# Adding the columns four apart on GpSimd instead of VectorE in a convolution with log-polar pooling, on one Trainium2 core

## What is computed

```python
# masks: 12 bins (2 radius levels x 6 angles) of a 9x9 window, each an average
y = conv(x per channel, masks)             # 12 pooled planes per channel
out = conv(planes arranged 4x3, w_conv1)   # = sum over channels and 12 bins
out = out + conv(x, w_center) + b_center
mean, var = out.mean((0, 2, 3)), out.var((0, 2, 3))
out = (out - mean) * rsqrt(var + 1e-5) * gamma + beta
return relu(out + x)
```

## Time and profile before

| | before |
|---|---|
| runs (3) | median 1686.37 us, 1686.28 to 1686.71 us |
| profiled execution, its own time | 1686.6 us |
| its span in the trace | 1684.8 us |
| mean granted TensorE clock | 0.949 |
| busy: PE / DVE / ACT / POOL | 1489.2 / 1531.3 / 645.3 / 2.7 us |
| phase 1 | to about 1533 us; phase 2 is the rest |

### The profile page before, as it was taken

The page is one execution under the profiler, slowest core; times in us unless marked ns, Lnnn a source line. Parts: engine busy times, 40 slices in busy tenths (PEclk is TensorE's granted clock), DMA queues, the critical chain, the costliest instruction groups (busy, mean ns, idle before and its releaser), DMA issues.

```text
span 1684.8 us, 21919 instructions
## 1 busy us (share of the span) xinstructions
PE 1489.2 (88%) x8468; PEld 1476.5 (88%) x8468; DVE 1531.3 (91%) x1455; ACT 645.3 (38%) x689; POOL 2.7 (0%) x21
## 2 busy tenths in 40 slices
PE   6899999999999999999999999999999999993000
PEld 6899999999999999999999999999999999993000
DVE  8999999999999999999999999999999999995423
ACT  3234343343333434334333343433433334434423
POOL 0000000000000000000000000000000000000000
PEclk8999999999999999999999999999999999997555
DMA  2010111001111011100111101111011110149999
GB/s 110 20 38 29 38 38 38 21 27 38 38 38 38 29 38 38 38 29 19 38 38 38 38 29 38 38 38 37 11 38 38 38 38 29 38 159 421 425 424 382
DMA packets 28615, 129.54 MB, mean 77 GB/s; under 512 B 3520, under 2 KB 3520, under 8 KB 28608
## 3 DMA queue, kind: packets, MB, share of 16 engines
q1 hardware_dynamic: 23744, 103.77, 17.0%
q10 hardware_dynamic: 4864, 25.69, 3.7%
HBM read 78.88 MB, written 50.58 MB: 77 GB/s over the span
## 4 chain that ended last, share of the span: by engine, by line
PE 50%; DVE 27%; issue 11%; SPq 5%; ACT 4%; DMA 3%; DVEq 0%; ACTq 0%
PE acc L625 17%; PE acc L627 16%; PE acc L626 16%; DVE pooled_split L403 6%; DVE pooled L402 6%; DVE inner_split L403 5%; SPq L266 3%; ACT inner_split L324 3%; DVE box L402 2%; DVE y_stage L402 2%; DVE row L402 2%; DMA phase<-x 2%; SPq L263 2%; DMA out<-phase 1%; ACT phase L394 0%
## 5 line engine op out<-in xcount | busy, mean ns | idle before, releaser
L334 ACT ACTIVATE pooled_split<-pooled 128x1456 fp32r<-128x1456 f32 x192 | 273.4, 1425 | 608.0 <-DVE pooled L402 608.0
L403 DVE TENSOR_TENSOR pooled_split<-pooled,pooled_split 128x1456 fp32r<-128x1456 f32 x192 | 317.4, 1667 | 0.3 <-ACT pooled_split L334 0.3
L625 PE MATMUL acc<-inner_split,w_first 128*128 128x406 f32 (+1 forms) x640 | 225.7, 353 | 36.3 <-DVE y_stage L402 25.0
L625 PE MATMUL acc<-pooled_split,w_first 128*128 128x364 f32 x768 | 253.6, 330 | 2.4 <-DVE pooled_split L403 2.4
L625 PE MATMUL acc<-pooled_split,w_outer 128*128 128x364 f32 x768 | 252.3, 329 | 1.1 <-DVE pooled_split L403 1.1
L626 PE MATMUL acc<-pooled_split,w_first 128*128 128x364 f32 x768 | 252.6, 329 | 0.0
L627 PE MATMUL acc<-pooled_split,w_first 128*128 128x364 f32 x768 | 252.5, 329 | 0.0
L626 PE MATMUL acc<-pooled_split,w_outer 128*128 128x364 f32 x768 | 252.2, 328 | 0.0
L627 PE MATMUL acc<-pooled_split,w_outer 128*128 128x364 f32 x768 | 251.8, 328 | 0.0
L627 PE MATMUL acc<-inner_split,w_first 128*128 128x406 f32 (+1 forms) x640 | 222.8, 348 | 0.0
L625 PE MATMUL acc<-inner_split,w_inner 128*128 128x406 f32 (+1 forms) x640 | 221.2, 346 | 1.1 <-DVE inner_split L403 1.1
(11 more groups left out here) (82 smaller groups left out, 2200.7 us busy)
## 6 DMA issues: line engine op xcount, KB each, us to landing
x_pad<-x SPq DMA_DIRECT2D x64, 392.0 KB, 3.3
y_dram<-y_stage SPq DMA_DIRECT2D x31, 784.0 KB, 5.0
phase<-y_dram SPq DMA_DIRECT2D x30, 784.0 KB, 28.3
phase<-x SPq DMA_DIRECT2D x30, 784.0 KB, 30.5
out<-phase ACTq DMA_DIRECT2D x30, 784.0 KB, 16.0
w_stage<-w_raw SPq DMA_DIRECT2D x2, 896.0 KB, 7.7
out<-x_pad ACTq DMA_DIRECT2D x2, 784.0 KB, 20.4
w_stage<-w_raw SPq DMA_DIRECT2D x2, 768.0 KB, 9.1
```

The costliest lines, as they stand in the source:

```text
L334: nc.scalar.activation(view(pooled_split, 2 * j * PAIR, (1, PAIR)), view(pooled, (PAIRS * c + j) % 2 * PAIR, (1, PAIR)), ACT.Copy)\
L403: sub = lambda out_, a, b: nc.vector.tensor_tensor(out_, a, b, ALU.subtract)
L625: nc.tensor.matmul(place, hi_w, hi_in, start=start, stop=False)
```

## The change

The add of the columns four apart leaves DVE's queue and stands in POOL's. There, add_ends waits for the image (x_loaded), for the short sums of the step before (pooled_ready, they read the tile ends), and for row3 of this step (row3_ready); then it adds and signals ends_ready. The semaphore x_used goes: SP's load of the next image waits for ends_ready in its place (row3 is the last of DVE's reads of x_pad in a step, so ends_ready, which comes behind row3_ready, covers them all). DVE's wait for ends_ready moves from before box4 to before the short sums.

```diff
--- before.py
+++ after.py
@@ -167,7 +167,6 @@
         zeroed = sem("zeroed")
         warmed_up = sem("warmed_up")
         x_loaded = [sem(f"x_loaded{c}") for c in range(CH)]
-        x_used = sem("x_used")
         d_ready = sem("d_ready")
         v_ready = sem("v_ready")
         inner_hi_ready = sem("inner_hi_ready")
@@ -232,6 +231,22 @@
                 nc.gpsimd.memset(edge, 0.0).then_inc(zeroed, 1)
                 n += 1
             assert n == ZEROED
+            pool.wait_ge(zeroed, ZEROED)
+
+            def add_ends(image):
+                for c in range(CH):
+                    s = CH * image + c
+                    first, second = (view(x_pad, c * X_PAD + (column + 2) * H, (H, W), (1, H)) for column in (-2, 2))
+                    pool.wait_ge(x_loaded[c], 16 * (image + 1))
+
+                    wait_from_one(pool, pooled_ready, PAIRS * s)
+                    pool.wait_ge(row3_ready, s + 1)
+                    nc.gpsimd.tensor_tensor(view(ends, 2, (ENDS_H, W), (1, H)), first, second, ALU.add)\
+                        .then_inc(ends_ready, 1)
+
+            add_ends(0)
+            with pool.Fori(1, IMAGES) as image:
+                add_ends(image)
 
         @block.sync
         def _(sp):
@@ -249,7 +264,7 @@
             def image_steps(image, first=False, last=False):
                 if not last:
                     for c in range(CH):
-                        sp.wait_ge(x_used, CH * image + c + 1)
+                        sp.wait_ge(ends_ready, CH * image + c + 1)
                         load_x(image + 1, c)
                 if not first:
                     sp.wait_ge(y_ready, CH * image + FREE)
@@ -533,8 +548,6 @@
                     dve.wait_ge(row2_ready, s + 1)
                     add(view(row3, 1, (ROW3_H, W + 2), (1, H)), view(row2, 4, (ROW2_H, W + 2), (1, H)),
                         columns(0, 1, W + 2)).then_inc(row3_ready, 1)
-                    add(view(ends, 2, (ENDS_H, W), (1, H)), columns(-2, 1, W), columns(2, 1, W))\
-                        .then_inc(ends_ready, 1)
 
                     dve.wait_ge(row3_ready, s + 1)
                     add(view(row3v, 2, (ROW3V_H, W + 2), (1, H + 1)), view(row3, 0, (ROW3_H, W + 2), (1, H + 1)),
@@ -550,8 +563,6 @@
                         if c == 0:
                             transform_weights(1)
 
-                    dve.wait_ge(ends_ready, s + 1)
-                    nc.vector.sem_inc(x_used, 1)
                     dve.wait_ge(row3v_ready, s + 1)
                     add(view(box4, 0, (BOX4_H, W + 2), (1, H + 3)), view(row3v, 0, (ROW3V_H, W + 2), (1, H + 3)),
                         view(row3v, 2, (ROW3V_H, W + 2), (1, H + 3))).then_inc(box4_ready, 1)
@@ -563,6 +574,7 @@
                     dve.wait_ge(box3_ready, s + 1)
                     pooled_sums(s, c, 1, box3, 4, 4 * BOX3_H - 4, BOX3_H, row2, 8, 5 * ROW2_H - 8, ROW2_H)
                     lo_of_pooled(s, c, 0)
+                    dve.wait_ge(ends_ready, s + 1)
                     short_sum(s, c, 0)
                     short_sum(s, c, 1).then_inc(pooled_ready, 1)
                     lo_of_pooled(s, c, 1)
```

## The result

The changed kernel takes 1748.15 us (median of 4 runs, 1748.0 to 1748.25) against 1686.36 us; the ratio is 1.037, with an interval of 1.035 to 1.038. It is slower by 61.8 us where 1745 was forecast. The profiled execution took 1748.0 us, its span is 1746.2 us.

The account below looks back on a forecast made before the run. A wait loop through PE and DVE bound the kernel at 46.72 us an image; DVE's own loop would take over at 48.57. 53.7 us over 29 periods plus 4.8 ahead, on 1686.6, gave 1745 us, range 1688 to 1773.

Parts of the forecast that it names:

- The mechanism: DVE's instructions with two SBUF inputs near row3v: each stands still for POOL's whole add, 1.5 to 2 us a step; chance 0.60.
- loop A: Image period through DVE, holding both steps' adds: 46.39 us before the change, forecast 48.57 after, then setting the pace.
- loop B: Image period through PE's wait for take_y, holding one step's add: 46.72 us and binding before, forecast 47.81 after.
- What is removed: The 64 adds of 0.969 us on DVE's queue: a step was to save 0.77 us, not 0.97.
- e: What DVE loses per POOL add, near row3v: forecast 1.86 us, between 0 and 2.31.
- hand-over: Passing between POOL and DVE at a stop: 0.12 us, counted once on top of POOL's 1.74 us add.
- The sum: Period 1.85 us longer, 53.7 us over 29 periods; 4.8 us ahead of them; 58.5 us together.
- head: The part ahead of 134.91 us, where DVE sets the pace in five steps: forecast 4.8 us longer.
- Rival 1: POOL's and DVE's SBUF reads go side by side, e = 0: period 45.95 us, 1660 us in all; chance 0.18.
- Rival 2: DVE's back-to-back reads keep POOL out until DVE waits for ends_ready: e = 1.98, 1753 us; chance 0.16.
- Rival 3: DVE is only slowed, e between 0.66 and 0.87, so the two moves cancel: 1686 us; chance 0.06.
- Waits and queues moved: add_ends's waits, SP's later load and store, DVE's moved wait for ends_ready: forecast to cost 0.

## Why the prediction was right, point by point

**The mechanism** was right in what it says of DVE: DVE is stopped by POOL's reading, in the place named (behind row3v), 1.5 to 2 us a step, and loop A takes over from loop B. What it left out is the clock. By the rule of the Trainium skill, "SBUF — State Buffer", section "Who interferes with whom", DVE with two SBUF inputs contends with a GpSimd instruction that reads, not with one that only writes, and a DVE instruction with at most one SBUF input, outside the modes that use both of its port pairs, doesn't contend. The runs agree on all three: 1.68 us with the add, 0 with the write, 0 beside the takes.

**What is removed** was right: row3 to row3v is 1.06 us (734.27 to 735.33), so a step saves 0.77.

**e** was forecast at 1.86 and is 1.68 + 0.07 = 1.75. POOL's own duration, forecast at 1.74, is 1.88 where nothing holds it; not all of it stops DVE. The skill's "GPSIMD Engine Reference", section 3.1, gave an estimated 1.72 by proportion, 8% under the 1.88 measured. The hand-over of 0.12 that I added is in no row. The 0.07 of the second wait ahead of the short sums is, and I had put that wait at nothing.

**Loop A** was overestimated. I took the idle of 0.34 us out of it, but an instruction that doesn't wait also overlaps the one before by 0.09, so without the wait the loop is 46.39 - 0.09 = 46.30. With that the measured stops give every period: 46.30 + 2 x (1.68 - 0.77 + 0.07) = 48.26 (measured 48.26); with DVE adding twice 46.30 + 2 x 0.885 = 48.07 (48.07).

**The sum.** 29 periods longer by 1.54 us are 44.7 us, where I had 53.7. The clock adds 8 x 1.55 = 12.4, where I had 0: I named it as what would bring the result above 1745 but gave it no price. The head gives 139.01 - 134.91 = 4.1, forecast 4.8; the stretch behind the last steady take_y 0.2, forecast 0. Together 61.4 us, the difference of the spans. So 1745 came out close by luck: two terms erred in opposite directions: e and loop A by 9.0 too much, the clock by 12.4 too little.

**Rival 1** (reads side by side, 1660 us) is refuted by the stops; its number, though, is the right floor within 2 us (1662.16 without an add), and an arrangement that keeps the reads apart nearly gets there. **Rival 2** didn't happen in the changed kernel; when the columns are halved, DVE's back-to-back reads do keep POOL out for seven instructions in every second step, though not until DVE waits for ends_ready. **Rival 3**, no change, didn't happen with the add; a copy of one operand, which is half of the reading, comes near it, with a stop of 0.65 us against the 0.77 saved, 1684.03 us.

**Waits and queues moved**: nothing but the 0.07 us a step above (the kernel without the add has a period of 46.03, loop B's 45.95 and this wait).

## What to carry to other kernels

Before an elementwise operation goes from VectorE to GpSimd, ask what VectorE runs at that moment: beside an instruction that reads two SBUF tiles the add here cost VectorE 1.68 us to save 0.77; beside one that reads PSUM and one SBUF tile it cost nothing, and where it ran over into the next it cost 0.15. Choose the semaphore that lets GpSimd go so that its reads fall beside such instructions, and the same move turned from 3.7% slower into 1.2% faster. And where a chain of waits makes TensorE stop for longer, the clock can add its own price to that of the stop: 12.4 of the 61.4 us here.

## What the runs showed of the hardware that was not expected

- PE's stops at take_y of 2.08 us in each image were followed by stretches at 1.2 GHz in 8 of 29 periods, 1.55 us each; stops of 1.88 us in 4 of 29; stops of 1.16 to 1.17 us and of 0.80 us in none. Work that nobody needs, put into the stops, made the kernel 12.5 us faster.
- POOL's add of 392 elements, let go in the same place, waited for one DVE instruction in one step and for seven in the next (1.28 and 8.38 us), in strict alternation over the whole steady stretch. So which engine gets the next turn doesn't follow from which came first; what decides it stays open.
- The stop of DVE is shorter than POOL's own duration (1.68 of 1.88 us), and reading one tile stops DVE for less than half of what two do (0.65).
